# Cross attention without a mask: weighing after each unit of scores, two units back, instead of after each pair

## The reference, cut to what matters

```python
def _L2_xattn_ref(x, context, context_mask, q_w, q_b, kv_w, kv_b, proj_w, proj_b):
    q = (x @ q_w + q_b).reshape(b, n, h, d)                 # 1024 tokens, 16 heads, d = 8
    kv = (context @ kv_w + kv_b).reshape(b, s, 2, h, d)     # 6404 context rows
    k = kv[:, :, 0]
    v = kv[:, :, 1]
    attn = jnp.einsum('bnhd,bshd->bhns', q, k) * scale
    attn = jnp.where(context_mask[:, None, None, :], -jnp.inf, attn)
    attn = jax.nn.softmax(attn, axis=-1)
    out = jnp.einsum('bhns,bshd->bnhd', attn, v).reshape(b, n, c)
    return out @ proj_w + proj_b
```

## Time and profile before

| what | value |
|---|---|
| median of three executions | 5569.26 us (5562.91 to 5574.53) |
| the profiled execution itself | 5570.45 us, its span 5568.7 us |
| mean granted TensorE clock over the span | 0.857 |
| busy over the span | PE 74%, DVE 65%, ACT 47%, POOL 14% |

### The profile page before, as it was taken

How to read it: one execution, slowest core, us unless ns; L and a number is a source line. 1 busy time by engine, 2 the same in 40 slices (tenths; PEclk the granted TensorE clock), 3 DMA queues, 4 the chain that set the end, 5 groups by cost and what they waited for, 6 DMA issues and landing times. The chain is left out here.

```text
span 5568.7 us, 98462 instructions
## 1 busy us (share of the span) xinstructions
PE 4142.3 (74%) x37512; PEld 1565.8 (28%) x37548; DVE 3597.7 (65%) x9663; ACT 2641.0 (47%) x3507; POOL 774.5 (14%) x990
## 2 busy tenths in 40 slices
PE   4956999853899999999855999999978575611114
PEld 2333444432322222222342222222224433300002
DVE  5554666576899989988246888888833566631213
ACT  2532666551366666666413888888871011100001
POOL 0000000002000000000003000000000003777772
PEclk7977999976699999999876999999999887855557
DMA  0020000053211122110014112112110500000000
GB/s 14 1 69 10 12 12 15 2 204 113 83 30 24 33 52 58 32 33 17 7 28 142 28 40 42 41 44 44 42 17 10 168 1 7 14 13 13 13 13 9
DMA packets 144187, 216.01 MB, mean 39 GB/s; under 512 B 52385, under 2 KB 106508, under 8 KB 141970
## 3 DMA queue, kind: packets, MB, share of 16 engines
q1 hardware_dynamic: 102106, 191.29, 12.5%
q0 software_dynamic: 20480, 10.53, 1.1%
q10 hardware_dynamic: 21128, 7.88, 0.6%
HBM read 160.66 MB, written 48.94 MB: 38 GB/s over the span
## 5 line engine op out<-in xcount | busy, mean ns | idle before, releaser
L1744 ACT ACTIVATE probs<-ps 128x1024 f32<-128x1024 f32 x1632 | 1594.5, 1023 | 450.2 <-PE ps L1684 445.1
L1799 DVE CUSTOM_DVE_ANT_0 junk<-ps,mask 128x512 bf16<-128x512 f32 (+1 forms) x1664 | 1056.7, 678 | 112.1 <-PE ps L1647 72.5
L1700 PE MATMUL ps<-probs,vstack 128*18 128x512 f32 x6528 | 880.1, 603 | 0.0
L1647 PE MATMUL ps<-kturned,qturned 49*64 49x512 bf16 (+3 forms) x5113 | 810.6, 393 | 59.0 <-DVE maxima L1799 21.1
L1799 DVE CUSTOM_DVE_ANT_0 junk<-ps,nothing 128x512 bf16<-128x512 f32 (+1 forms) x1080 | 686.8, 672 | 125.6 <-PE ps L1647 123.9
L3443 POOL DMA_INDIRECT line<-table,index x640 | 619.7, 968 | 678.4 <-DVE index L3816 483.6
L1684 PE MATMUL ps<-qturned,kturned 53*64 53x512 bf16 x6528 | 626.3, 396 | 16.3 <-ACT probs L1744 7.2
L1647 PEld LDWEIGHTS ps<-kturned,qturned 49*64 49x64 bf16 (+1 forms) x5113 | 216.6, 103 | 899.6 <-issue 408.6
L3570 PE MATMUL ps<-ident,attended 128*128 128x128 f32 x8 | 3.8, 474 | 512.3 <-DVE attended L3840 512.3
L1671 PE MATMUL ps<-maskT,split 64*128 64x512 bf16 x1632 | 321.8, 384 | 0.0
L1684 PEld LDWEIGHTS ps<-qturned,kturned 53*64 53x64 bf16 x6528 | 186.9, 105 | 411.1 <-issue 256.3
(11 more groups left out here) (736 smaller groups left out, 5345.6 us busy)
## 6 DMA issues: line engine op xcount, KB each, us to landing
vstack<-values_heads SPq DMA_DIRECT2D x128, 229.5 KB, 4.9
mask_raw<-in_mask_BxSxS_if SPq DMA_DIRECT2D x8, 3202.0 KB, 17.6
kturned<-keys_parts SPq DMA_DIRECT2D x384, 54.0 KB
kturned<-keys_parts SPq DMA_DIRECT2D x384, 48.0 KB
table<-lines SPq DMA_DIRECT2D x51, 256.0 KB, 3.1
line<-table,index POOLq DMA_INDIRECT x640, 2.3
keys_parts<-parts SPq DMA_DIRECT2D x24, 384.0 KB, 2.6
kapart<-keys_apart SPq DMA_DIRECT2D x160, 48.0 KB
```

Source lines behind the costliest of these rows:

```text
L1647: last = nc.tensor.matmul(ring(e)[part, 0:hi - lo], qturned[rows, h % 3, m * P + part.start:m * P + part.stop], src, start=True, stop=True ...
L1700: last = nc.tensor.matmul(k.ps[at:at + PAIR, 4, :], vstack[:, h % 2, first, t, :], probs[:, (h * KT + t) % slots, first, :], start=(t < 2) ...
L1744: nc.scalar.activation(probs[:, u % slots].rearrange("p b n -> p (b n)"), k.ps[:, bank:bank + 2, :].rearrange("p b n -> p (b n)"), ACT.Exp ...
L1799: nc.vector.tensor_tensor_reduce(junk[:, at % RING, 0:hi - lo], ring(e)[:, 0:hi - lo], lost, 1.0, -3.0e38, ALU.subtract, ALU.max, maxima[: ...
```

## The change

In the plain call (`singly`, where there is no `maskT`) the list holds for each unit: its scores, its pieces, the weighing of the unit two back. A weighing step has one unit (two matmuls), and there are 51 in a round. All pieces of the plain call are cut into 64x64 tiles, those ahead of the first unit too. `COPIED` takes a=1 for all four chunks, so the copied piece is always the second of its couple. ACT's exponential of a unit comes ahead of the copies of its pieces. The masked call keeps its list.

```diff
-WEIGHS = KT // 2 + 1
-COPIED = {0: 0, 4: 1, 6: 0, 10: 1}
+COPIED = {0: 1, 4: 1, 6: 1, 10: 1}
...
     late = {}
+    if singly:
+        for u in range(HALVES * KT):
+            late.setdefault(u + 2, []).append(("weigh", u // KT, u % KT))
+        for h in range(HALVES):
+            late.setdefault((h + 1) * KT + 3, []).append(("sums", h))
+        for u in range(HALVES * KT):
+            out += [("scores", u)] + spread[u] + late.pop(u, [])
+        for u in sorted(late):
+            out += late[u]
+        return out
...
+    singly = maskT is None
+    together = 1 if singly else 2
+    weighs = -(-KT // together)
+    steps = programme(singly)
...
-                ts = range(2 * i, min(2 * i + 2, KT))
+                ts = range(together * i, min(together * (i + 1), KT))
...
-            parts = whole
+            parts = quarters if singly else whole
...
-                    for u in (e[1], e[1] + 1):
+                    for u in range(e[1], e[1] + together):
```

More of the change, by code:

```diff
@@ L1427, in both_of, with programme @@
     return [[("piece", h, i), ("piece", h, i + 1)] for i in range(first, last, 2)]
-def programme():
+def programme(singly):
     n = len(pieces())
@@ L1444, in programme @@
     late = {}
+    if singly:
[8 more added lines that the diff above has]
+        return out
     for h in range(HALVES):
-        for i in range(WEIGHS):
+        for i in range(KT // 2 + 1):
             late.setdefault((h * KT + min(2 * i + 1, KT - 1)) // 2 + 1, []).append(("weigh", h, i))
@@ L1460, in cross @@
     slots = 6
-    steps = programme()
+    singly = maskT is None
+    together = 1 if singly else 2
+    weighs = -(-KT // together)
+    steps = programme(singly)
     ring_at, last_piece = {}, {}
@@ L1524, in weighs_with @@
         def weighs_with(u):
-            return WEIGHS * (u // KT) + u % KT // 2 + 1
+            return weighs * (u // KT) + u % KT // together + 1
         @block.sync
@@ L1592, in _ @@
                 keys(h, 1)
-                sp.wait_ge(weighed, WEIGHS * (h - 1))
+                sp.wait_ge(weighed, weighs * (h - 1))
                 values(h)
@@ L1721, in _ @@
                 elif e[0] == "behind_weighing":
-                    parts = whole if maskT is not None else quarters
+                    parts = whole
                 elif e[0] == "behind_scores":
@@ L1754, in ahead @@
                 nc.scalar.activation(twins[:, twin[e] % TWINS, :], ring(e), ACT.Relu).then_inc(ring_free[ring_at[e] % RING], 1)
-            following = 1
             for e in steps:
                 if e[0] == "scores":
[L1759 to L1765, removed]
+                    for u in range(e[1], e[1] + together):
+                        exponentials(u)
                 elif e in twin:
@@ L1770, in _ @@
                     nc.scalar.copy(qturned[:, e[1] % 3, :], ring(e).bitcast(BF16)[:, 0:BANK]).then_inc(ring_free[ring_at[e] % RING], 1)
-                elif e[0] == "weigh" and e[2] == WEIGHS - 1:
+                elif e[0] == "weigh" and e[2] == weighs - 1:
                     h = e[1]
-                    act.wait_ge(weighed, WEIGHS * (h + 1))
+                    act.wait_ge(weighed, weighs * (h + 1))
                     if h >= 2:
```

## The result

The changed kernel takes 5812.76 us (median of four executions), the kernel before on the same chip 5566.09: slower by 246.7 us, ratio 1.0441 with a 95% interval of 1.0414 to 1.0467. One of the four executions of the changed kernel took 6178 us, at a lower clock (0.753, the others 0.870 to 0.873); it is in this median and not in the ratio, and without it the median is 5808.3 us, +242.2. Forecast were 5803 us and +233. The profiled execution has a span of 5815.3 us.

The account below looks back on a forecast made before the run. Before, PE, ACT and DVE tie in the plain call; after, PE alone bounds it. Unit terms sum to 1304.3 us against 1071.3, +233.0; added to the profiled 5570.45 this gives 5803 us, range 5750 to 5855.

Parts of the forecast that it names:

- The weighing block: Plain call on PE: a block of two matmuls costs 0.97 us, one of four 0.98; blocks go from 416 to 816.
- No waits in ordinary units: Plain call, units with one couple of pieces: PE takes 1.53 us without waiting; earlier waits of 0.46 us a pair go.
- Units with two couples: 42 plain-call units whose second couple waits for the ring: 1.75 + 0.97 = 2.72 us each, in all 114.2 us.
- The sum: PE's time over the plain call's 816 units, first scores to last weighing: 1304.3 us against 1071.3, +233.0 us.
- the x20 block: Last weighing block of the plain call, 2.76 us: read as three units in turn and expected to stay that.
- The order of the copied pieces: Copied piece second of its couple, plain call: removes waits the slower pace has already removed, so counted as nothing.
- a tie of PE, ACT and DVE: Plain call before: three engines close together, PE's fixed work about 2.05 of 2.51 us a pair, the rest waiting.
- Price by matmuls: Rival: a weighing block of two matmuls costs half of four, 0.49 us; ACT then bounds the call, 5476 us; chance 0.03.
- Switch free: Rival: scores and pieces begin while the weighing drains, so 155 us go: +78, 5648 us; chance 0.05.
- Waits stay: Rival: PE still waits 0.23 us a unit for ring or exponentials, 188 us on top: 5991 us; chance 0.06.
- Pieces cut in two ahead of the first unit: 104 + 12 pieces before the first unit, cut in two: counted as nothing, -12 us at best if the clock rose earlier.

Follow-up runs that it names:

- Filled strips: Changed kernel with each unit's weighing matmuls issued twice, so that all four column strips are used: 5825.43 us, ratio 1.0459 to the kernel before.
- half the columns: Changed kernel with the plain call's weighing over 256 of the 512 tokens of a round: 5524.97 us, ratio 0.9914 to the kernel before.
- the old order with cut blocks: Changed kernel with the list of before, each block of four weighing matmuls cut into two blocks of one unit: 5791.97 us, ratio 1.0393.
- the order with the weighing one back: Changed kernel's unit by unit order, weighing two units together, the block one unit earlier (`+ 1` for `+ 2`): 5701.28 us, ratio 1.0225.

## Why the prediction was right, and where it was not

- **The weighing block** (forecast 0.97 us a unit, 816 blocks): 0.97 us. Filled strips, half the columns and the old order with cut blocks show separately that two matmuls cost what four do, that 0.86 us of it is streaming, and that this alone makes the old order nearly as slow (219 of 240 us). This step is shown.
- **No waits in ordinary units, 1.53 us**: right, in the rows above. ACT and DVE idle 335 and 334 us, nearly all of it for PE.
- **Units with two couples** (1.75 us from scores to weighing, taken from the masked call): the second couple waits as there. The timeline after:

```profile
3103.45 0.40 PE L1659 MATMUL ps<-kturned,qturned 49*64 49x512 bf16 x2
3104.37 0.40 PE L1659 MATMUL ps<-kturned,qturned 49*64 49x512 bf16 x2 [0.51 <-DVE maxima L1805]
3104.70 1.04 PE L1712 MATMUL ps<-probs,vstack 128*18 128x512 f32 x4
```

- **The sum** (1304.3 us from first scores to last weighing): 1311.4. By the same terms a round in the middle of the call takes 83.0 us, and from first scores to first scores 83.1 was measured, so the sum is right in its parts and not only in total. Some 4 of the 7 us missing are the first four units, which ran at the 1.2 GHz level and took 9.4 us (3073.72 to 3083.08) where 5.4 were summed. I had the clock row for the stretch before and left out that it reaches into the call. The other 6.5 us of the result lie outside the call, 5.8 of them before the masked call begins; that start varied by 12 us among the kernels of this study (1510 to 1522 us), so I put nothing on them. One reading in the sum was wrong without harm: the x20 block of the earlier trace rows is five units (two pairs and a single one) and not three, and it did not stay as it was; after, the last block is x12 and 2.24 us.
- **"The order of the copied pieces ... I give it nothing"**: for the forecast of the whole this did no harm, since the second of the couple is what the changed kernel has. As a statement it was wrong. I worked out the ring's latency for a piece that DVE reads (free in time), and not for one that ACT copies after a 1.03 us exponential. The table alone is worth 39 us of the call in the new order, and nothing in the old.
- **"So PE has some 0.46 us of waiting in a pair, for the ring of pieces and for exponentials: the call runs as a tie of PE, ACT and DVE"**: the size was right and the waits went, as forecast. The cause was named too loosely. In the rows the wait is the fourth piece's, for DVE's reading of the first, a link of a chain that runs through PE and DVE and fills the 2.51 us; the call is no tie of sums there, though DVE's four readings come within a few hundredths of it. With two pieces between two blocks the changed kernel has no fourth piece, except in the units with two couples.
- **The rivals.** Price by matmuls: refuted by the filled strips. Switch free: refuted, the steps into and out of a block are 0.32 and 0.97 in every ordinary unit of the rows. The Trainium skill, TensorEngine Tiling (Array Packing), section Key Properties, has it that a change of tiling mode drains the array; the trace agrees, since the scores behind a block with two idle strips start at most 0.01 us sooner than behind a filled one (0.97 and 0.98 us). Waits stay: refuted by the rows.
- **Pieces cut in two ahead of the first unit**: forecast nothing. The granted clock there stayed 0.50 and both traces spend about 60 us from the first piece to the first scores. This part of the change was not run by itself.

## What to carry to other kernels

When a matmul uses a fraction of the array's columns, as the weighing does here, look whether its tiles are issued together: here a block of two cost what a block of four did, so count blocks, not matmuls, and look in the trace for the odd remainder of a loop, since it shows what a half-filled block costs. Before reordering for one engine, follow one period from each wait to what ended it, across the engines, and add up the steps: busy shares of 94, 87 and 79% looked like a tie, and the period was a chain through a ring of three banks. A reorder that leaves as many pieces between two blocks leaves that chain as it is. Check a ring's latency for every reader, the slow one first.

## What the runs showed of the hardware that I had not expected

In the last round of the order with the weighing one back, the granted clock fell to the 1.2 GHz level after five pairs of 2.52 us in each of which PE paused 0.91 us, and it stayed down for the 64 us to the round's end, with pauses of 0.70 us in pairs of 3.62 us. In that round of the changed kernel, where PE was busy 63.6 of 64 us (4320 to 4384), it stayed at 1.00. What made the clock fall after the fifth such pair and not before stays open, and so does what brought on the short falls in seven of the rounds before it.
